# A new order of scan, drive and product on VectorE, with decays one pair earlier on ScalarE and the Silu table asked for ahead of each wait

## The reference

```
x = conv_block(x)          # mixture of 4 experts: expand 96->576, 5x5 depthwise, squeeze and excite, 576->96
x = x + mamba(group_norm(x))   # the scan below
t = t + fourier_mixer(ln(t));  t = t + ffn(ln(t))      # t: 784 tokens of 96
t = t + linear_attention(ln(t)); t = t + ffn(ln(t))
```

```
h[n]  = exp(delta * A[n]) * h[n] + (delta * u) * B[n]     # per channel d, state n, along 784 positions
y     = sum over n of h[n] * C[n]
```

## Time and profile before

| what | value |
|---|---|
| median of 3 runs | 22538.34 us (22494.2 to 22542.6) |
| profiled execution | 22505.68 us, span from first to last instruction 22503.9 us |
| TensorE busy | 18818.0 us, 84% of the span |
| VectorE busy | 19251.1 us, 86% |
| ScalarE busy | 15624.5 us, 69% |
| GpSimd busy | 6356.1 us, 28% |
| mean granted TensorE clock | 0.894 |

### The profile page before, as it was taken

How to read it: one execution, slowest core, us unless ns; L and a number is a source line. 1 busy time by engine, 2 the same in 40 slices (tenths; PEclk the granted TensorE clock), 3 DMA queues, 4 the chain that set the end, 5 groups by cost and what they waited for, 6 DMA issues and landing times.

```text
span 22503.9 us, 334261 instructions
## 1 busy us (share of the span) xinstructions
PE 18818.0 (84%) x100834; PEld 6890.1 (31%) x100834; DVE 19251.1 (86%) x17938; ACT 15624.5 (69%) x21098; POOL 6356.1 (28%) x3909
## 2 busy tenths in 40 slices
PE   5888888888888888888888888888888888888887
PEld 1333333333333333333333333333333333333332
DVE  4888888888888888888888888888888888888887
ACT  3767777777677677776776777767767767777674
POOL 1222222222222222222222222222222222222222
PEclk8889898898898998988988889889889898898898
DMA  5555555555555555555555555545555555555552
GB/s 144 143 135 140 140 138 139 135 144 137 132 142 138 137 142 135 143 138 134 140 141 133 140 136 141 140 133 143 138 133 143 139 139 141 134 142 136 134 141 75
DMA packets 1418366, 3083.16 MB, mean 137 GB/s; under 512 B 207812, under 2 KB 786696, under 8 KB 1407859
## 3 DMA queue, kind: packets, MB, share of 16 engines
q1 hardware_dynamic: 1372146, 2992.85, 51.6%
q10 hardware_dynamic: 44032, 64.26, 1.1%
HBM read 2796.25 MB, written 221.51 MB: 134 GB/s over the span
## 4 chain that ended last, share of the span: by engine, by line
issue 67%; POOL 15%; PE 8%; DVE 5%; ACT 4%; DMA 1%; POOLq 0%; ACTq 0%; SPq 0%; DVEq 0%
POOL drive L1576 13%; PE bank L575 3%; DVE state L1381 3%; PE state_sum L575 2%; PE pair L575 2%; POOL taps L1563 2%; ACT work L920 1%; DVE drive L1237 1%; PE scan_sum L575 1%; ACT L920 0%; ACT decay_even L920 0%; DVE work L1237 0%; ACT du L920 0%; DVE prod L1237 0%; ACT decay L920 0%
## 5 line engine op out<-in xcount | busy, mean ns | idle before, releaser
L1576 POOL TENSOR_TENSOR drive<-du,Bb 128x784 f32<-128x784 f32 x3072 | 5689.7, 1852 | 15638.6 <-DVE drive L1237 15638.6
L575 PE MATMUL state_sum<-state,fold 128*64 128x392 f32 x24576 | 5610.5, 585 | 1052.4 <-DVE state L1381 1029.9
L1381 DVE TENSOR_TENSOR_SCAN state<-decay_even,drive 128x784 f32<-128x784 f32 x3072 | 5500.2, 1790 | 128.4 <-ACT decay_even L920 17.6
L1381 DVE TENSOR_TENSOR_SCAN state<-decay,drive 128x784 f32<-128x784 f32 x3072 | 5473.3, 1782 | 0.2 <-POOL drive L1576 0.2
L920 ACT ACTIVATE decay_even<-delta,alog 128x784 f32<-128x784 f32 x3072 | 2821.6, 918 | 3240.8 <-DVE state L1381 3224.0
L1237 DVE TENSOR_TENSOR prod<-state_sum,Cb 128x784 f32<-128x784 f32 x3072 | 2950.6, 960 | 1906.4 <-PE state_sum L575 1902.4
L575 PE MATMUL scan_sum<-prod,fold 128*64 128x392 f32 x12288 | 2990.4, 568 | 1500.0 <-DVE prod L1237 1493.9
L575 PEld LDWEIGHTS state_sum<-state,fold 128*64 128x64 f32 x24576 | 1706.4, 154 | 4427.8 <-issue 2288.4
L575 PE MATMUL bank<-rep,taps 120*32 120x392 f32 x30720 | 2973.9, 514 | 96.1 <-ACT image L920 33.8
L920 ACT ACTIVATE decay<-delta,alog 128x784 f32<-128x784 f32 x3072 | 2890.3, 941 | 115.6 <-issue 72.7
L1237 DVE TENSOR_TENSOR drive<-du,Bb 128x784 f32<-128x784 f32 x3072 | 2943.0, 958 | 18.9 <-DVE work L1237 11.9
(11 more groups left out here) (169 smaller groups left out, 17504.8 us busy)
## 6 DMA issues: line engine op xcount, KB each, us to landing
Bb<-bc_rows SPq DMA_DIRECT2D x3072, 392.0 KB, 4.4
rep<-expanded_images SPq DMA_DIRECT2D x3840, 168.0 KB
Cb<-bc_rows SPq DMA_DIRECT2D x3072, 196.0 KB, 3.6
expanded_images<-image SPq DMA_DIRECT2D x1152, 112.0 KB, 2.5
rep<-conv_in_images SPq DMA_DIRECT2D x1152, 112.0 KB, 3.9
dwo<-in_pww SPq DMA_DIRECT2D x65, 1152.0 KB, 7.3
conv_in_images<-image SPq DMA_DIRECT2D x384, 112.0 KB, 3.2
xc<-xc ACTq DMA_DIRECT2D x384, 98.0 KB, 2.6
```

The source lines that it names most:

```text
L575: return pe.matmul(out, lhsT, rhs, start=start, stop=stop)
L1381: v.tensor_tensor_scan(state[:, j % STATES, :], DP[:, 0:L] if j % 2 == 0 else decay[:, j // 2 % DECAYS, :], drive[:, j % 2, :], 0.0, ALU.m ...
L1576: pool.tensor_tensor(drive[:, j % 2, :], du[:, 2 * s + r, :], Bb[:, b % BSLOTS, :], ALU.mult).then_inc(drive_r.sem, 1)
```

## The change

VectorE's order for pair p becomes: even scan, visits, even drive of pair p+1, odd scan, product of pair p-1, visits. The first even drive of a sample is made during the last pair of the sample before. There are four state buffers in place of three. VectorE's even drive now waits also for the odd drive of GpSimd (`drive_r`), and GpSimd's odd drive for the scan that read the buffer.

TensorE's order becomes: folds of pair p, visits, summation of pair p-1, visits. ScalarE's decays run one pair ahead, across the border of two samples. `gates()` asks for the Silu set ahead of the wait of a Silu. The bias of squeeze and excite goes into TensorE as a matmul with the identity, so that the Sigmoid reads PSUM and `scp` falls away. The group norm's power goes from GpSimd to ScalarE as Ln and Exp, with a third small ScalarE instruction for the shift. Many places move: expand 3 goes ahead of the first convolution, the mix of experts for the next sample from places 79 and 80 to 91 and 93, the far deltas from slots 4, 6, 16, 22 to 8, 12, 22, 25, and many pieces of the tail one place later.

```diff
-STATES = 3
+STATES = 4
-CONV_SLOTS = (1, 2, 3, 5, 7, 8, 9, 10, 11, 12, 13, 14, 15, 17, 18, 19, 20, 21, 23, 24, 26)
+CONV_SLOTS = (1, 2, 3, 4, 6, 7, 9, 10, 11, 13, 14, 15, 16, 17, 18, 19, 20, 21, 23, 24, 26)
-             ("mix", 0): 79.1, ("mix", 1): 80.3, ("dbl",): 81.1,
+             ("mix", 0): 91.1, ("mix", 1): 93.1})
-FAR = {("delta", m, h): slot(k) + SECOND * h for m, k in ((2, 4), (3, 6), (4, 16), (5, 22)) for h in range(2)}
+FAR = {("delta", m, h): slot(k) + SECOND * h for m, k in ((2, 8), (3, 12), (4, 22), (5, 25)) for h in range(2)}
...
 # TensorE
             def scan(i, *between):
                 for p in range(NP):
-                    if p >= 1:
-                        summation(i, p - 1)
-                    elif later(i):
-                        summation(i - 1, NP - 1)
-                    go_on(between, 2 * p + 1)
                     pe.wait_ge(state_r.sem, state_r.at(i, 2 * p + 2))
                     if p >= 1 or later(i):
                         pe.wait_ge(prod_r.sem, prod_r.at(i, p))
...
                     last.then_inc(folded.sem, 1)
                     go_on(between, 2 * p + 2)
+                    if p >= 1:
+                        summation(i, p - 1)
+                    elif later(i):
+                        summation(i - 1, NP - 1)
+                    go_on(between, 2 * p + 3)
...
 # ScalarE
+            def gates():
+                if table[0] != SILU:
+                    act.preload_act_table_set(SILU)
+                table[0] = SILU
...
             def convolved(i, span, t, h):
                 yield READ_AT["conv", t, h]
                 m = 2 * t + h
+                gates()
                 act.wait_ge(bank_filled.sem, bank(span, "conv", t, h))
...
+            def scan(i, ahead, *between):
+                for j in range(2, NU + 2 if ahead else NU, 2):
+                    for n in (j, j + 1):
+                        if n < NU:
+                            decaying(i, n)
+                        else:
+                            decaying(i + 1, n - NU)
+                        go_on(between, j - 1.5 if n == j else j - 1)
...
             def gating(i, b):
-                yield 2.95 + 2 * b
+                yield 3.6 + 2 * b
+                gates()
...
 # VectorE
-                def driving(j):
+                def driving(i, j):
...
                     if j >= 2 or later(i):
+                        v.wait_ge(drive_r.sem, drive_r.at(i, j))
                         v.wait_ge(state_r.sem, state_r.at(i, j - 1))
...
                 for p in range(NP):
-                    driving(2 * p)
                     scanning(2 * p)
+                    go_on(between, 2 * p)
+                    if p < NP - 1:
+                        driving(i, 2 * p + 2)
+                    elif ahead:
+                        driving(i + 1, 0)
+                    scanning(2 * p + 1)
                     if p >= 1:
                         product(i, p - 1)
                     elif later(i):
                         product(i - 1, NP - 1)
-                    go_on(between, 2 * p)
-                    scanning(2 * p + 1)
                     go_on(between, 2 * p + 1)
...
 # GpSimd
                 pool.wait_ge(drive_r.sem, drive_r.at(i, j))
+                if j >= 2 or later(i):
+                    pool.wait_ge(state_r.sem, state_r.at(i, j - 1))
```

More of the change, by code:

```diff
@@ L388, in build, with decay_of @@
         lmax = w[2][:, 8:8 + NB]
+        def decay_of(j):
+            return decay[:, j // 2 % DECAYS, :] if j % 2 else DP[:, 0:L]
         def u_of(m):
@@ L847, in attention @@
                 yield ATTN_AT
-                pe.wait_ge(o_r.sem, o_r.at(i, 2))
-                yield from norm(i, ATTN_AT, 2, o_r, (2, 2))
+                pe.wait_ge(o_r.sem, o_r.at(i, 1))
+                yield from norm(i, ATTN_AT, 2, o_r, (1, 2))
                 yield ATTN_AT + 4
@@ L1049, in logs @@
             def logs(i, span):
-                yield from log_exp(i, span, 0)
-                yield from log_exp(i, span, 1)
-                yield from log_of(i, 0)
-                yield from log_of(i, 1)
+                for m in range(NEAR):
+                    yield from log_exp(i, span, m)
+                    yield from log_of(i, m)
             def far_logs(i, span):
@@ L1058, in far_logs, with decaying @@
                     yield from log_of(i, m)
[L1060 to L1078 removed]
+            def decaying(i, j):
+                s, m, r = PAIRS[j // 2]
+                k, n = 2 * s + r, 2 * m + j % 2
+                exponentials()
+                if m == 0:
+                    act.wait_ge(dl_r.sem, dl_r.at(i, k + 1))
+                back, signal = (2 * DECAYS, odd_r) if j % 2 else (2, even_r)
+                if j >= back or later(i):
+                    act.wait_ge(state_r.sem, state_r.at(i, j - back + 1))
+                ac(decay_of(j), delta[:, k, :], ACT.Exp, scale=alog[:, k, n:n + 1]).then_inc(signal.sem, 1)
+            def scan(i, ahead, *between):
[6 more added lines that the diff above has]
+                        go_on(between, j - 1.5 if n == j else j - 1)
                 go_on(between, END)
@@ L1354, in steps, with scan @@
                     tt(du[:, m, :], delta[:, m, :], u_of(m), ALU.mult).then_inc(du_r.sem, 1)
-            def scan(i, *between):
+            def scan(i, ahead, *between):
                 def product(i, p):
@@ L1380, in scanning @@
                     v.wait_ge(drive_r.sem, drive_r.at(i, j + 1))
-                    v.tensor_tensor_scan(state[:, j % STATES, :], DP[:, 0:L] if j % 2 == 0 else decay[:, j // 2 % DECAYS, :], drive[:, j % 2, :], 0.0,
+                    v.tensor_tensor_scan(state[:, j % STATES, :], decay_of(j), drive[:, j % 2, :], 0.0,
                                          ALU.mult, ALU.add).then_inc(state_r.sem, 1)
@@ L1528, in _ @@
             go_on([Beside(lead(0, (FIRST, 0))), Beside(shares(1))], END)
-            scan(0, Beside(steps(0, NEAR, NK)), Beside(lead(1, (LOOP, 0))), Beside(shares(2)))
+            scan(0, True, Beside(steps(0, NEAR, NK)), Beside(lead(1, (LOOP, 0))), Beside(shares(2)))
             done = SETUP_LINKS + 2 * LEAD_LINKS
```

192 lines of the change are left out of this document (93 added, 99 removed).

## The result

The changed kernel takes 23327.0 us (median of 4 runs, 23265.4 to 23385.2) against 22540.5 us (4 runs) of the kernel before on the same chip: a ratio of 1.0358, 95% interval 1.0339 to 1.0378. The forecast was 21380 us, 5% faster; its range ended at 22200. Its sign is wrong.

What follows compares the result with a forecast made beforehand. VectorE (86% busy) and TensorE (84%) bound the kernel, VectorE waiting at the product. 31.5 - 7.8 - 3.8 - 4.0 + 2.0 = 17.9 us a sample, times 63 is 1128, from 22505.7 to 21380 us; range 20600 to 22200.

Steps and rivals of the forecast that it cites:

- The product's wait: VectorE's idle time before the product, ended by TensorE's folds: 1906.4 us, 29.8 us a sample, was to fall.
- the 700 named: Sign of a right forecast: idle time before the product falls from 1906 to under 700 us.
- the slack of 3 us: At the product of each pair, TensorE may be late by 3.0 us in the new order, in place of 1.2.
- The floors: Nine stretches of a sample, each at TensorE's or VectorE's larger busy time: 313.4 us, 31.5 under today's 344.9.
- Idle time put back: In the five stretches that VectorE bounds, half of its 7.6 us idle time stays: 3.8 us a sample.
- Waits that are added: VectorE's even drive for GpSimd, GpSimd for the odd scan, later C rows on SyncE's queue: all costed at nothing.
- The sign I had named for it: A late SyncE queue, costed at nothing, would show as waits for DMA.
- Tables: ScalarE's table loads rise from 53 to 59 a sample, worst in pairs 3 to 5: 4 us put back.
- The clock: TensorE's granted clock in pairs 5-9 and 35-43 nears 0.95 with fewer waits: 2 us a sample won.
- The rival GpSimd: GpSimd's odd drive beside VectorE's odd visits slows them, 5.8 us a sample: 21740 us, chance 0.07.
- The slower rival: ScalarE's even decay comes late behind convolution reads, 27 us a sample: 23080 us, chance 0.08.
- Chances: Whole kernel: faster 0.90, same 0.02, slower 0.08; the forecast itself had 0.68.

Runs made afterwards that it cites:

- three runs on places and tables: Changed kernel with, singly: near delta's matmul moved behind the norm's, 23157.8 us; input projection at old places, 22993.3; no early Silu load, gates at old places, 23190.1.
- first two edits: Changed kernel with VectorE's visits only behind the even scan and its even drive ahead of them: 22679.8 us, ratio 1.0072.
- the run with 55 a sample: Changed kernel with no Silu load ahead of waits and the tail's three gates back at their old places: 23190.1 us, ratio 1.0310.
- the four edits: Changed kernel: visits only behind even scan, even drive ahead; delta's matmul behind norm's; projection at old places; no early Silu load, old gate places: 22048.9 us, ratio 0.9797.
- VectorE's old order and mended places: Changed kernel with the delta's matmul, projection, and Silu-load and gate edits kept, VectorE in the order of the kernel before: 22782.0 us, ratio 1.0118.

## Why the prediction was wrong, step by step

*The product's wait.* Right: 1906 to 344 us, under the 700 named. The reading of the one pair and of the slack of 3 us held.

*The floors.* This step failed: "the floor of a stretch is the larger one of TensorE's and VectorE's busy time". It takes everything but busy time for removable. A stretch also has chains that hop between VectorE, ScalarE and TensorE (norm, attention, layer norm), and each hop waits for its place in the next engine's list. In pair 43 this is to be seen link by link. The kernel before had these chains too, with VectorE standing still for 30 us a sample at the product while the other engines worked. The three runs on places and tables (160, 310 and 108 us) and their sum with the first two edits show that the lost time sits there. That it was the product's wait that hid the chains before, one run shows in part: with VectorE in the old order, and its product waiting again, the visits' waits for TensorE are 7.6 us a sample (15.1 in the changed kernel, 7.8 before), but those for ScalarE still 11.5 (16.2, 2.0).

*Idle time put back.* The term was 3.8 us a sample, half of 7.6. What came is 14.2 + 7.3 + 4.1 us at visits and the bare wait. This step failed as well, by a term that stood at nothing: the places that move, "many pieces of the tail one place later", and the projection's two places got no price at all. The projection's alone is 310 us, and with the delta's and the tables it is 540 us (VectorE in the old order). I counted only moves that shift busy time between stretches, not moves that shorten the distance between a result and its use.

*Waits that are added.* The even drive hardly waits for GpSimd, as said. It does stand behind a visit's bare wait for ScalarE, 4.1 us a sample, which I had not looked for, though I asked what stands behind the waiting drive. B rows and image stores were to be "used more than a pair (5.5 us) after their issue"; the rows of images, which are loaded from those stores, are late by 340.8 and 210.1 us a run, where it was 29.6 and 4.5. The sign I had named for it, waits for DMA, is there; the cause, in the case of the 210, is the projection's later place and not SyncE's queue. Of the 340.8 the old places of the lead's first half take away only 90; the rest stays open.

*Tables.* 59 loads a sample were forecast, and so it is in samples 20 to 29 (53 before; 3728 / 64 = 58.3 over the whole run). The price of 4.0 us for six more was rather high: the run with 55 a sample gives 108 / 63 = 1.7 us for four of them, which would be 2.5 for six; the intervals leave room up to 4. The stretch named, pairs 3 to 5, is where it lies (pairs 0 to 4 lose 5.7 us), with the layer norm's wait on top.

*The clock.* +2 us were expected from fewer waits; the mean is 0.890 (0.894 before). In the samples shown pairs 5 to 9 went from 0.91 to 0.95 as said, pairs 35 to 43 from 0.89 to 0.81, a mixture of stretches at 2.4 and at 1.2 GHz (0.87 to 0.92 and 0.92 to 0.86 as means over samples 20 to 29). In pair 43 TensorE stands idle for 2.09 us at once and then runs at 0.51; with one matmul moved this idle time is gone, the pair stays at 1.00, and the variance matmul takes 1.56 in place of 2.93 us. So clock was lost there along with the wait, where the prediction counted only with a gain: TensorE's same 100962 matmuls take 18653.9 us in that run and 18821.3 in the changed kernel. In the run with the four edits the mean is 0.915.

*The rival GpSimd.* Its place was right, its price rule wrong. I had 0.64 us for each us of overlap, 5.8 us a sample; VectorE's busy time, which the sum took as unchanged, grew by 7.5. It is a hold: 378 of the 768 casts start while GpSimd works, and each of them ends 0.22 or 0.23 us after GpSimd's instruction, however long that goes on. The Trainium skill, SBUF — State Buffer, section "SBUF: two separate sides", gives an exclusive lock for the whole instruction and no split, against VectorE instructions with two SBUF inputs or in a 2-port mode. The trace agrees on the lock; in which mode a cast runs no run here shows. The odd scan of the earlier trace rows fits as well: held for 0.39 us, it was longer by 0.25, and the cast shown, held for 1.15 us, by 1.03. As a cause of time the hold is worth some 153 us, not 365: most of it lay in front of waits.

*The slower rival.* Its 23080 is the nearest of all the times given, for a reason that is hardly there. The even decays hold the scan by 273 us and the odd ones by 133, 6.4 us a sample, not 27; with the visits only behind the even scan the even ones alone come to 626.7 us, still under 10 a sample. Its idea, that a chain over ScalarE and TensorE comes late when TensorE's pieces move behind folds, is the right one; I applied it to the decay, and it struck the norms and attention.

*Chances.* 0.90 for faster came from cases that all had the same step in common, the floors. A mechanism that all cases share is not made safer by their number.

*Open.* With VectorE's old order and mended places the kernel is still 1.2% slower than before; its norms wait 308.6 us for ScalarE there (33.9 before), and the places behind that were not tried one by one. With the four edits pairs 10 to 18 still take 66.4 us (57.4 before; pairs 5 to 9 give 6.1 of that back). TensorE's new order, folds ahead of the summation, was not tried alone. Nor was a later place for the bare waits on VectorE.

## What to carry to other kernels

Before an idle time of the fullest engine is counted as gain, ask which other chains run in its shadow: each result that another engine makes during that wait needs a new place when it goes. In kernels whose engines run fixed lists, price every moved place by the distance between a result and its use, and look on the queue that carries two streams for an instruction that waits in front of one that is ready. A change that comes out slower may hold a good core: here five edits to VectorE's order, to places and to tables, tried one by one, bring the ratio from 1.0358 down to 0.9797.

## What was unexpected of the hardware

- GpSimd's 784-column drive (1.85 us) stops VectorE instructions until it has ended: casts of 128x392 from f16 to fp8 took 1.18 us on average beside it and 0.34 us elsewhere, and additions and multiplications with both operands in SBUF went the same way (the residual's addition 548 to 1062 ns as a group's mean). The product and the even scan, each with one operand in PSUM, kept their 0.95 and 1.78 us beside it, and GpSimd's drive kept its own time (1852 and 1856 ns).
- The hold is no loss by itself: cut away, it gave back 604 us of VectorE's busy time and 153 us of the kernel's.
- TensorE's work took 18821 us in the changed kernel and 18332 us in the version with the four edits, with the same 100962 matmuls; the mean granted clock was 0.89 and 0.915. In one pair the granted clock was 0.51 behind 2.09 us of idle TensorE, and 1.00 when one matmul had been moved and that idle time was gone.
